# A routed vision tower on one core: routing every five chunks, normalising moved to VectorE, tile 0 fetched within the shared network, padding cut to the ends of the regions

## The chip, the core and the metric

The kernel runs on one core of a Trainium2 chip. The metric is the device time of one execution in microseconds. Before the change three runs gave 1068.31, 1070.25 and 1070.76 us: the median is 1070.25.

## What is computed

64 images of 3 x 96 x 96 are cut into 36 patches each; with a class token that makes 37 tokens of width 256 an image, 2368 in all. Two layers follow (no skip beyond those written):

```
h  = embed(patches) + pos                      # 768 -> 256
h  = h + attn0(norm(h))                        # 16 heads, causal, relative bias
x  = norm(h)
h  = h + shared(x) + sum over the 2 best of 7 experts of w_e * expert_e(x)   # SwiGLU, hidden 704
h  = h + attn1(norm(h))
h  = h + ffn1(norm(h))                         # SwiGLU, hidden 768, int8-like weights
```

The weights w of the two experts are the two largest softmax probabilities, divided by their sum. Everything is held in 32-bit floats; most products are made of three matmuls of an upper and a lower half of each operand (mm3).

## The kernel before, in words

The kernel is a hand-written program for each engine; each engine runs its own list in order, and semaphores join them. Work goes over 8 groups of 8 images (N = 296 tokens). The stages are: embedding; attention(0); ffn(0), the shared network, with the routing woven in; routed(), 43 tiles of 128 routed rows, one expert each; attention(1); ffn(1).

**ffn(0).** A group has six chunks of hidden units (five of 128, one of 64), counted j = 0 to 5. For a chunk, TensorE computes gate and up (gate_up), ScalarE the SiLU (Sg) and later the upper half of the product, VectorE the product (Hd) and the lower half (Hf_lo), and TensorE adds the down product of the chunk two back (LAG = 2). In groups 0 to 6 the routing of the next group, g + 1, is spread over the six chunks: TensorE logits (L1354), token_rows (L1362), counts (L1371); VectorE route (L904, five pieces of small linked operations) and slots_of (L939); ScalarE r_exp and rows, which copy the tokens with their weight into the row buffers rows_x. At the same time the normalisation of group g + 2 runs: mean (TensorE), centre (VectorE), squares (ScalarE), variance (TensorE), deviation (ScalarE, between two activation table loads), norm (L406, GpSimd: xn), then upper_x (ScalarE) and lower_x (L411, GpSimd). The positions are MEAN_AT and VARIANCE_AT (L56).

**The scatter.** For each group GpSimd runs scatter (L485): eight indirect writes of 74 token rows (256 values, the weight, the number of the target row) into routed_in (xs) in DRAM, in the region of each token's expert. A region has room for all tokens. Since a tile of 128 rows may reach past the last row of its expert, SP first fills all of routed_in with rows that count for nothing (L332, nine transfers), behind the loads of the embedding; the first scatter waits for them. In the last group VectorE computes the table of the tiles (table_of_tiles, L1113: expert and first row of each tile) from the counts.

**The queues.** SP's list is: inputs, shared weights, the fill, expert 4 (when the embedding is done), experts 0 to 3 (when attention(0) is done), then a wait for all scatters and the table, then the loads of the tiles (xt, L356), tile t + 2 when tile t has been used. ScalarE issues the loads of experts 5 and 6 and of the weights of attention(1) after tile 0's upper_in (L854 to L856).

**The start of routed().** TensorE waits for the last add to h (L1748), runs six matmuls that compute nothing (keep_going, L1728), transposes tile 0 (tile_in, L1686), and starts its gate and up. Each tile needs the upper half of its expert's weights (ScalarE, upper_weights, L824) and the lower half (VectorE, lower_weights, L1204); their buffers lie over those of the normalisation, so both wait for the end of ffn(0) (norms_idle) and of the scatters (rows_idle). The loop then does, for each tile t: gate and up of half 0, the transpose of tile t - 1's hidden, half 1, tile_in of t + 1, tile_out of t - 1.

```
step(0, 0, True, True, False)                 # over_groups, L286
...
link = linker(RCHAIN * g)                     # route: every operation waits for the one before
```

## Time and profile before

| | us |
|---|---|
| median of three runs | 1070.25 |
| profiled execution, device time | 1067.98 |
| its span | 1066.1 |
| TensorE busy | 982.8 (92%) |
| VectorE busy | 646.8 (61%) |
| ScalarE busy | 624.5 (59%) |
| GpSimd busy | 375.3 (35%) |

The stages in the span: embedding and attention(0) to about 250 us, ffn(0) to 404, the passage and the first tiles to 430, the tiles to 738, then attention(1) and ffn(1). In the profile, PE is TensorE's matmuls and PEld its weight loads, DVE is VectorE, ACT ScalarE, POOL GpSimd, SP the engine that only issues transfers. A row of a timeline has the start, the duration, the engine, the line, the operation, output and inputs, the count, and in brackets how long the engine had been idle before and what released it. The granted clock of TensorE is 1.00 at its upper level (2.4 GHz) and 0.50 at its lower (1.2 GHz).

### The profile page before, as it was taken

Reading aid. Unit: us, or ns where it says so; the run is one execution under the profiler, and the core shown is the slowest. Engines: PE = TensorE matmul, PEld = TensorE weight load, DVE = VectorE, ACT = ScalarE, POOL = GpSimd, SP = SyncE. Lnnn points to the kernel's source line nnn. Section 1 sums busy time; section 2 is a strip of 40 time slices with the busy share of each in tenths; the row PEclk is TensorE's granted clock in tenths of the full one; section 3 lists DMA queues with packets and bytes.
Section 4 is the critical chain, followed back from the end, with each engine's and each line's share of the span. In section 5 each row is a group of like instructions: output and inputs, shape, how many; then the busy total and the mean of one; then the engine's idle time right before and its main releaser. Section 6 shows DMA issues by size and latency. Waiting matters only on the chain.

```text
span 1066.1 us, 28004 instructions
## 1 busy us (share of the span) xinstructions
PE 982.8 (92%) x10628; PEld 891.4 (84%) x10629; DVE 646.8 (61%) x1207; ACT 624.5 (59%) x1077; POOL 375.3 (35%) x295
## 2 busy tenths in 40 slices
PE   4987799988899996999999999999799999899998
PEld 4976688877899995999999999998678888689998
DVE  3635467775666665667667676672467776654543
ACT  3345476864556654565656656653376778655652
POOL 1343334454777770111111111112554654711210
PEclk9998899998999999999999999999899999999999
DMA  6799900005411116011111111111611100000000
GB/s 230 258 246 248 246 17 3 3 3 234 144 35 32 37 37 233 30 40 33 36 35 35 40 35 35 40 34 54 171 26 26 26 2 2 3 13 12 24 24 24
DMA packets 47517, 74.71 MB, mean 70 GB/s; under 512 B 13138, under 2 KB 38994, under 8 KB 46268
## 3 DMA queue, kind: packets, MB, share of 16 engines
q1 hardware_dynamic: 32288, 55.55, 18.7%
q0 software_dynamic: 13328, 10.66, 3.7%
q10 hardware_dynamic: 1804, 7.11, 1.7%
q8 instruction: 72, 1.18, 0.5%
q14 instruction: 25, 0.20, 0.1%
HBM read 41.47 MB, written 31.71 MB: 69 GB/s over the span
## 4 chain that ended last, share of the span: by engine, by line
PE 74%; DVE 6%; issue 6%; ACT 6%; POOL 5%; DMA 3%; SPq 0%; DVEq 0%; ACTq 0%; POOLq 0%
PE ps L1303 24%; PE ps L1308 14%; PE ps L1310 13%; PE ps L1309 13%; POOL routed_in L504 3%; PE ps L1708 3%; PE ps L1452 3%; PE ps L1441 2%; DMA x_in<-in_xT_dram 1%; PE ps L1691 1%; DVE Hd L1103 1%; DVE hsum L1093 1%; DMA xt<-routed_in 1%; ACT RTs L668 1%; ACT RTs L666 1%
## 5 line engine op out<-in xcount | busy, mean ns | idle before, releaser
L1206 DVE TENSOR_TENSOR tile_w<-arena,tile_w 128x1408 fp32r<-128x1408 f32 x86 | 139.5, 1622 | 77.2 <-ACT tile_w L828 77.2
L528 POOL DMA_INDIRECT routed_out<-yt,tile_to x43 | 41.2, 959 | 295.0 <-DVE yt L1228 295.0
L1308 PE MATMUL ps<-tile_w,xTs 128*128 128x352 f32 x344 | 118.8, 345 | 2.6 <-DVE xTs L1211 2.6
L1303 PE MATMUL ps<-arena,shared 128*128 x516 | 120.0, 383 | 1.0 <-ACT shared L822 1.0
L828 ACT ACTIVATE tile_w<-arena 128x1408 fp32r x86 | 118.6, 1379 | 3.3 <-issue 1.5
L1310 PE MATMUL ps<-tile_w,xTs 128*128 128x352 f32 x344 | 111.7, 325 | 0.0
L1309 PE MATMUL ps<-tile_w,xTs 128*128 128x352 f32 x344 | 111.5, 324 | 0.0
L1303 PEld LDWEIGHTS ps<-arena,shared 128*128 128x128 f32 x516 | 95.8, 192 | 12.8 <-issue 1.3
L815 ACT ACTIVATE shared<-ps 128x352 f32<-128x352 f32 x86 | 39.7, 461 | 112.6 <-PE ps L1310 112.6
L398 POOL TENSOR_TENSOR Km<-KT,cst 128x592 f32<-128x592 f32 x64 | 75.6, 1183 | 75.6 <-PE ps L1303 51.8
L969 DVE SCALAR_TENSOR_TENSOR ps<-ps,bias 128x592 f32<-128x592 f32 x64 | 50.1, 783 | 60.2 <-PE ps L1303 60.2
L1103 DVE TENSOR_TENSOR Hd<-Sg,ps 128x296 f32<-128x296 f32 x96 | 44.4, 462 | 68.8 <-ACT Sg L781 67.9
L1308 PE MATMUL ps<-xf_hi,gu_lo 128*128 128x296 f32 x272 | 82.4, 303 | 3.4 <-DVE Hd L1103 2.1
L775 ACT ACTIVATE Hf_hi<-Hd 128x296 fp32r<-128x296 f32 x96 | 43.3, 452 | 71.1 <-DVE Hd L1103 71.1
L1309 PE MATMUL ps<-xf_lo,gu_hi 128*128 128x296 f32 x272 | 81.8, 301 | 0.0
L1310 PE MATMUL ps<-xf_hi,gu_hi 128*128 128x296 f32 x272 | 81.7, 300 | 0.0
L408 POOL TENSOR_TENSOR xn<-cen,rsd 128x592 f32<-128x592 f32 x31 | 45.4, 1463 | 102.1 <-ACT rsd L605 102.0
L654 ACT ACTIVATE prs<-Sb 128x592 f32<-128x592 f32 x64 | 44.7, 698 | 53.9 <-DVE Sb L982 53.8
L1308 PEld LDWEIGHTS ps<-tile_w,xTs 128*128 128x128 f32 x344 | 65.1, 189 | 10.0 <-issue 4.5
L1108 DVE TENSOR_TENSOR Hf_lo<-Hd,Hf_hi 128x296 fp32r<-128x296 f32 x96 | 47.5, 495 | 42.4 <-ACT Hf_hi L775 42.4
L781 ACT ACTIVATE Sg<-ps 128x296 f32<-128x296 f32 x96 | 39.6, 412 | 53.2 <-PE ps L1310 52.3
L1308 PE MATMUL ps<-xa_hi,qkv_p_lo 128*128 128x296 f32 x192 | 66.0, 344 | 2.5 <-DVE h L1010 2.5
(199 smaller groups left out, 2819.0 us busy)
## 6 DMA issues: line engine op xcount, KB each, us to landing
routed_in<-zero_x SPq DMA_DIRECT2D x8, 2064.0 KB, 28.0
arena<-in_ew_dram SPq DMA_DIRECT2D x5, 2176.0 KB, 18.8
x_in<-in_xT_dram SPq DMA_DIRECT2D x7, 888.0 KB, 5.9
xt<-routed_in SPq DMA_DIRECT2D x43, 129.0 KB
arena<-in_ew_dram ACTq DMA_DIRECT2D x2, 2176.0 KB, 10.4
yg<-routed_out SPq DMA_DIRECT2D x8, 512.0 KB
out_dram<-h SPq DMA_DIRECT2D x8, 296.0 KB, 2.7
routed_in<-zero_x SPq DMA_DIRECT2D x1, 1806.0 KB, 27.8
```

Source lines behind the costliest of these rows:

```text
L398: pool.tensor_tensor(Km[p % 2], src, headmask.unsqueeze(1).unsqueeze(3).to_broadcast([P, DK, HG, W2]), ALU.mult).then_inc(a.km, 1)
L408: pool.tensor_tensor(xn[b][:], cen[:], rsd[:].unsqueeze(1).to_broadcast([P, DK, N]), ALU.mult).then_inc(s.xn, 1)
L654: act.activation(Pr[p % 2], Sb[p % 2], ACT.Exp).then_inc(a.ex, 1)
L828: act.activation(tile_w[half][0], gate_up_of(w, half), ACT.Copy).then_inc(s.wh, 1)
L969: dve.scalar_tensor_tensor(out=ps[:, 0:2, 0:DK * HW], in0=ps[:, 0:2, 0:DK * HW], scalar=HD ** -0.5, in1=halves_of(bias[l][:]), op0=ALU.mul ...
L1103: dve.tensor_tensor(Hd[j % (LAG + 1)][0:r], Sg[j % 2][0:r], up, ALU.mult).then_inc(s.hd, 1)
L1108: dve.tensor_tensor(lower, Hd[j % (LAG + 1)][0:r], upper.bitcast(F32), ALU.subtract).then_inc(s.hl, 1)
L1206: dve.tensor_tensor(tile_w[half][1], gate_up_of(w, half), tile_w[half][0].bitcast(F32), ALU.subtract).then_inc(s.wl, 1)
L1303: return pe.matmul(out_, lhsT, rhs, start=start, stop=stop)
L1308: pe.matmul(out_, w[1], x[0], start=start, stop=False)
L1309: pe.matmul(out_, w[0], x[1], start=False, stop=False)
L1310: return pe.matmul(out_, w[0], x[0], start=False, stop=stop)
```

## The change

The routing no longer follows the groups. routing_at(g, j) numbers the chunks of ffn(0) through: routing r (1 to 7) takes chunks 5r - 4 to 5r, one fifth each, so that all are done at chunk 35 of 0 to 47. Within it, the normalisation of group r + 1 runs. norm and lower_x of ffn(0) go from GpSimd to VectorE; GpSimd only scatters, and then issues the loads of experts 5 and 6. The table is computed in group 6; its first piece now also writes ends, the counts as row numbers. The fill becomes six blocks of 128 rows for the spare tiles (five on SP, one on GpSimd) and, when the final counts (ends) are known, seven blocks of 128 rows, each behind the last row of an expert. SP then loads tiles 0 and 1 within the last group; TensorE transposes tile 0 there at j = 3, behind the down product, ScalarE makes its upper half at j = 4, VectorE its lower half at the end. keep_going(6) is gone; the last add to h stands behind the first lower_weights. Cut to its core:

```diff
-MEAN_AT, VARIANCE_AT = (2, 0), (4, 3)
+MEAN_AT, VARIANCE_AT = 0, 3
+PACE = 5
...
+        def routing_at(g, j):
+            at = len(hidden_chunks(I0)) * g + j - 1
+            return (1 + at // PACE, at % PACE) if 0 <= at < PACE * (GROUPS - 1) else (None, None)
@@ SP @@
-            for r in range(0, ROWS, FILL * P):
-                rows = min(FILL, (ROWS - r) // P)
-                sp.dma_start(xs[r:r + rows * P, :].rearrange("(p k) d -> p k d", p=P),
-                             zero_x[:].unsqueeze(1).to_broadcast([P, rows, XW])).then_inc(s_pad, 16)
+            for k in range(1, SPARE):
+                r = EXPERTS * REGION + k * P
+                sp.dma_start(xs[r:r + P, :], zero_x[:]).then_inc(s_pad, 16)
...
-            for scattered in s_scat:
-                sp.wait_ge(scattered, 64 * GROUPS)
+            sp.wait_ge(s_ends, 1)
+            for e in range(EXPERTS):
+                row = sp.value_load(ends[0:1, e:e + 1], min_val=0, max_val=ROWS - P)
+                sp.dma_start(xs[bass.ds(row, P), :], zero_x[:]).then_inc(s_pad, 16)
+            rows_idle(sp)
+            sp.wait_ge(s_pad, 16 * (EXPERTS + SPARE - 1))
+            sp.wait_ge(s_exl, 16)
             sp.wait_ge(s_table, 1)
@@ GpSimd @@
+            def ffn0():
+                pool.dma_start(xs[EXPERTS * REGION:EXPERTS * REGION + P, :], zero_x[:]).then_inc(s_exl, 16)
+                for g in range(GROUPS):
+                    scatter(F[0], g, g % 2)
+                pool.wait_ge(F[0].dn_mm, LAG + 1 + 6 * GROUPS)
+                for e in range(EARLY, EXPERTS):
+                    pool.dma_start(arena[:, e * EW:(e + 1) * EW], ew[e]).then_inc(s_exl, 16)
@@ ScalarE, ffn(0): called with routing_at(g, j) after each chunk @@
+                def routing(r, at):
+                    if at == 2:
+                        sent_before(act, r)
+                        rows(r, r % 2, 0, 7)
+                        if r + 1 < GROUPS:
+                            squares(s, r + 1)
+                    if at == 3:
+                        act.preload_act_table_set("natural_log_exp_and_others")
+                        if r + 1 < GROUPS:
+                            deviation(s, r + 1, 6)
+                        r_exp(r)
+                    if at == 4:
+                        rows(r, r % 2, 1, 7)
...
+                        if l == 0 and last and j == 4:
+                            upper_in(0, 0)
@@ ScalarE, routed @@
                 norms_idle(act)
+                rows_idle(act)
                 w = weights_of(act, 0)
                 upper_weights(0, w, 0)
-                rows_idle(act)
                 upper_weights(0, w, 1)
-                upper_in(0, 0)
-                act.wait_ge(F[0].dn_mm, LAG + 1 + 6 * GROUPS)
-                for e in range(EARLY, EXPERTS):
-                    act.dma_start(arena[:, e * EW:(e + 1) * EW], ew[e]).then_inc(s_exl, 16)
-                act.dma_start(qkv_w1, qkv1).then_inc(s_attw, 16)
-                act.dma_start(out_w1, wo1).then_inc(s_attw, 16)
                 w = weights_of(act, 1)
                 gate(0, 0)
                 upper_weights(1, w, 0)
                 upper_in(1, 1)
                 gate(0, 1)
                 upper_weights(1, w, 1)
+                act.dma_start(qkv_w1, qkv1).then_inc(s_attw, 16)
+                act.dma_start(out_w1, wo1).then_inc(s_attw, 16)
@@ VectorE, ffn(0) @@
+                def norm(g):
+                    dve.wait_ge(s.rsd, FREE + g + 1)
+                    dve.wait_ge(s.cen, FREE + g + 1)
+                    dve.wait_ge(s.xl, g - 1)
+                    dve.tensor_tensor(xn[g % 2][:], cen[:], rsd[:].unsqueeze(1).to_broadcast([P, DK, N]),
+                                      ALU.mult).then_inc(s.xn, 1)
+                def lower_x(g):
+                    x = xf[0][g % 2]
+                    dve.wait_ge(s.xh, g + 1)
+                    dve.tensor_tensor(x[1], xn[g % 2][:], x[0].bitcast(F32), ALU.subtract).then_inc(s.xl, 1)
...
+                def routing(r, at):
+                    if at == 4:
+                        if r + 1 < GROUPS:
+                            norm(r + 1)
+                        slots_of(r, r % 2)
+                    next(routes[r])
+                    if at == 1 and r + 1 < GROUPS:
+                        dve.wait_ge(s.xn, FREE + r + 1)
+                        centre(s, r + 1, 6)
...
+                        if l == 0 and g == GROUPS - 2 and j < TABLE_PIECES:
+                            next(pieces)
+                        if l == 0 and not last and j == 3:
+                            lower_x(g + 1)
@@ VectorE, after ffn(0) @@
-                add_y(GROUPS - 1)
+                if l == 0:
+                    tile_in(0, 0)
...
                 norms_idle(dve)
+                rows_idle(dve)
                 w = weights_of(dve, 0)
                 lower_weights(0, w, 0)
-                rows_idle(dve)
-                tile_in(0, 0)
+                add_y(0, GROUPS - 1)
                 lower_weights(0, w, 1)
@@ TensorE, ffn(0), after gate_up of chunk j @@
+                        if at == 1 and r + 1 < GROUPS:
+                            pe.wait_ge(s.r, RCHAIN * (r - 1) + ROUTE + SLOTS)
+                            mean(s, r + 1, 6)
...
+                        if at == 0:
+                            pe.wait_ge(s.rowB, FREE + r)
+                            logits(r, r % 2, 7)
+                        if at == 1:
+                            pe.wait_ge(s.lg, FREE + r + 1)
+                            token_rows(r, r % 2, 0, 7)
+                        if at == 3:
+                            pe.wait_ge(s.rowA, FREE + r + 1)
+                            token_rows(r, r % 2, 1, 7)
+                            if r + 1 < GROUPS:
+                                pe.wait_ge(s.cen, FREE + r + 2)
+                                variance(s, r + 1, 6)
+                        if at == 4:
+                            pe.wait_ge(s.lnv, FREE + min(r + 2, GROUPS))
+                            counts(r)
+                        if l == 0 and last and j == 3:
+                            pe.wait_ge(s.r, RCHAIN * GROUPS)
+                            tile_in(0, 0, 0)
@@ TensorE, routed @@
-                keep_going(6)
-                tile_in(0, 0, 0)
                 gate_up_half(0, 0, 0)
```

The upper and lower half of tile 0, which lay in the shared network's weights, move to the place of the bias of attention(0).

## Rows read from the trace of the kernel before

**Rows 1.** The chain that ended last, share of the span by engine.

```profile
PE 74%; DVE 6%; issue 6%; ACT 6%; POOL 5%; DMA 3%; SPq 0%; DVEq 0%; ACTq 0%; POOLq 0%
```

**Rows 2.** Windows in attention(0): length; busy of PE, PEld, DVE, ACT, POOL; PEclk, DMA, GB/s.

```profile
120.00:140.00 20.00, 14.85 (x288) 12.07 (x287) 9.61 (x17) 9.51 (x20) 6.44 (x5) 0.91 0.75 189
...
126.00:128.00 2.00, 2.00 (x34) 1.64 (x26) 0.89 (x2) 1.56 (x4) 0.44 (x1) 0.50 1.43 184
...
140.00:160.00 20.00, 19.43 (x398) 16.40 (x398) 14.34 (x25) 14.21 (x28) 9.04 (x7) 1.00 0.01 3
```

**Rows 3.** Timeline of ScalarE, attention(0): the first PTs copy of groups 0, 3 and 4.

```profile
74.26 0.67 ACT L660 ACTIVATE PTs<-ps 74x592 f32<-74x592 f32 x1 [0.82 <-PE ps L1452]
...
149.19 0.67 ACT L660 ACTIVATE PTs<-ps 74x592 f32<-74x592 f32 x1
...
168.68 0.65 ACT L660 ACTIVATE PTs<-ps 74x592 f32<-74x592 f32 x1
```

**Rows 4.** Timeline of TensorE, attention(0): first, longest and last of ten gaps.

```profile
72.81 0.72 PE L1303 MATMUL ps<-Km,QT 64*37 64x148 f32 x16 [1.25 <-issue]
...
124.50 0.67 PE L1303 MATMUL ps<-Km,QT 64*37 64x148 f32 x10 [3.13 <-issue]
133.24 0.25 PE L1303 MATMUL ps<-PTs,cst 74*32 74x74 f32 x1 [1.62 <-issue]
```

**Rows 5.** DMA issues: count, size of each, median us to landing.

```profile
routed_in<-zero_x SPq DMA_DIRECT2D x8, 2064.0 KB, 28.0
```

**Rows 6.** Window of one steady group of ffn(0), columns as in rows 2.

```profile
323.00:342.00 19.00, 19.00 (x146) 18.00 (x145) 11.89 (x39) 11.68 (x21) 14.56 (x13) 1.00 0.17 34
```

**Rows 7.** Timeline of TensorE, ffn(0): the three stalls within it.

```profile
268.13 0.67 PE L1303 MATMUL ps<-rt,cst 74*74 74x28 f32 x8 [1.41 <-DVE rt L927]
...
275.60 1.20 PE L1303 MATMUL ps<-r_w,xn 128*74 128x7 f32 x16 [1.49 <-POOL xn L408]
...
401.36 0.40 PE L1308 MATMUL ps<-Hf_hi,dn_lo 128*128 128x296 f32 x1 [1.07 <-DVE Hf_lo L1108]
```

**Rows 8.** Timeline of the passage from ffn(0) to the tiles.

```profile
403.62 0.30 PE L1310 MATMUL ps<-Hf_hi,dn_hi 128*128 128x296 f32 x1
403.63 1.38 ACT L828 ACTIVATE tile_w<-arena 128x1408 fp32r x1 [1.34 <-issue]
...
405.50 1.62 DVE L1206 TENSOR_TENSOR tile_w<-arena,tile_w 128x1408 fp32r<-128x1408 f32 x1 [0.47 <-ACT tile_w L828]
...
411.03 0.43 PE L1308 MATMUL ps<-tile_w,xTs 128*128 128x352 f32 x1 [1.03 <-DVE xTs L1211]
...
418.51 0.40 PE L1308 MATMUL ps<-tile_w,xTs 128*128 128x352 f32 x1 [1.60 <-DVE xTs L1211]
...
425.65 0.69 PE L1691 MATMUL ps<-cst,xt 128*128 128x128 f32 x2 [2.41 <-DMA xt<-routed_in]
...
430.00 0.51 PE L1308 MATMUL ps<-tile_w,xTs 128*128 128x352 f32 x1
```

**Rows 9.** Timeline of VectorE, ffn(0): a lower half beside a pass of GpSimd.

```profile
265.73 1.94 DVE L1108 TENSOR_TENSOR Hf_lo<-Hd,Hf_hi 128x296 fp32r<-128x296 f32 x1 [0.52 <-ACT Hf_hi L775]
```

**Rows 10.** Timeline of ffn(0), 360 to 372 us: subtraction of the mean, Sg, lower half.

```profile
360.88 0.77 DVE L877 TENSOR_TENSOR cen<-h,ps 128x592 f32<-128x592 f32 x1
...
365.17 0.40 ACT L781 ACTIVATE Sg<-ps 128x296 f32<-128x296 f32 x1
...
371.99 0.48 DVE L1108 TENSOR_TENSOR Hf_lo<-Hd,Hf_hi 64x296 fp32r<-64x296 f32 x1 [0.52 <-ACT Hf_hi L775]
```

**Rows 11.** The scatters by tile (ns min/median/max), and the chain from the last one.

```profile
L504 POOL DMA_INDIRECT routed_in<-prs,slot x32: 1343/1354/1747, 259.1 to 386.3; - x32
...
401.05 5.29 DMA routed_in<-vts,slot
406.34 0.02 SPq L351
...
407.37 2.15 DMA xt<-routed_in
```

## What I expect, and why

> **What bounds the kernel now.** I began with the chain that ended last: TensorE holds 74% of it [rows 1], so time goes only where TensorE waits or runs slowly. I therefore went through the stages and looked for such places.
>
> The first is attention(0). From 120 to 140 us TensorE is busy 14.85 of 20 us and the granted clock is 0.91; from 140 to 160 it is busy 19.43 at a full clock, and the DMA share drops from 0.75 to 0.01 [rows 2]. The PTs copies of ScalarE mark the groups of attention(0): the first starts at 74.26, the fourth at 149.19, the fifth at 168.68 [rows 3]. A steady group thus takes 19.5 us, and the first three took 74.9 where 58.5 would do: 16.4 us are lost. Ten gaps of 0.4 to 3.1 us on TensorE, from 72.81 to 133.24, stand in that stretch with "issue" as releaser: no engine, no data [rows 4]. They sum to 14.3 us, and stretches at the lower of the two clocks (0.50, that is 1.2 GHz) follow them [rows 2]. What fills the DMA engines is the padding of routed_in: eight writes of 2 MB [rows 5] and a ninth, somewhat smaller.
>
> The second place is ffn(0). A steady group takes 19.0 us with TensorE busy throughout [rows 6]. TensorE stalls only at three places: 1.41 and 1.49 us around the first group and 1.07 us at the tail [rows 7].
>
> The third is the passage from ffn(0) to the experts' tiles. The last shared matmul starts at 403.62; tile 0 starts at 411.03, tile 1 at 418.51, tile 2 only at 430.00, after 2.41 us of waiting for its rows [rows 8]. From tile 2 on the loop is full, and the change leaves it alone.
>
> **Part 1, the padding.** 18 MB of writes become 13 blocks of 129 KB; one goes on the GpSimd queue, and seven wait for the final counts. With the DMA engines idle, as from 140 us on, attention runs at 19.5 us a group, so up to 16.4 us return. One gap probably stays: the load of expert 4, until now behind the padding on SP's queue, moves forward to about 70 us, and the last gap (1.62 us) came while that load ran [rows 4]. Sum: -15. Bounds: -9 (the gaps less that one and a low-clock stretch in exchange) to -19 (the first group has no output projection and should take less than 19.5).
>
> What the gaps wait for is not named by the trace. The Trainium skill (Runtime: NRT & Kernel Launch, Instruction fetch mechanics) says that instructions stream in by a DMA queue of the sequencer, in blocks of 16 KiB, at a cost that is "mostly hidden". By its last word this part would give about nothing; that is a rival below. Rows 2 and 4 speak for the gaps going with the traffic.
>
> **Part 2, the rhythm of the routing.** Seven routings of five chunks fill chunks 1 to 35. TensorE's work stays the same: the same logits, transposes, counts, six means and six variances. What can change are its waits.
> Gone: VectorE no longer shares its time with GpSimd's passes. A lower half took 1.94 us instead of 0.47 beside one [rows 9], and this delayed the counts (1.41); the logits' 1.49 was a wait for xn, which GpSimd made behind its scatters [rows 7]. That is -2.9. The table leaves the last group, so the tail's 1.07 shrinks by 0.8.
> New: xn is made on VectorE after the chunk's lower half. Before, this chain ran beside it. From one Sg (365.17) through the table loads to the end of the lower half of the next chunk (372.46) took 7.3 us [rows 10]; with the normalising pass, priced as the 128x592 subtraction (0.77, [rows 10]), 8.1. The copy of rows and the squares in the chunk ahead make ScalarE start some 0.6 late: 8.7. TensorE comes to the next logits after 60 matmuls, at 146 in 19.0 us [rows 6] 7.8 us later. So it waits 0.9 us in each of six rounds, and about 0.8 more in the two where a short chunk lies between; a 128x592 copy for the next x adds some 0.7 in one or two. That sums to 8; the two chunks of lag between gate/up and down absorb part of it, and I take +6. Bounds: 0 (the lag covers all) to +12 (2 us a round, by the larger stalls above).
> VectorE itself fits: of 19.0 us it is busy 11.9 [rows 6]. It gains two 0.77 passes, loses the locked time, and the round shrinks to 16.7 (19.0 less one chunk). GpSimd fits with room: eight scatters at 1.35 and 0.3 between, 13.2 us, and about 2 for the tokens.
>
> **Part 3, tile 0 inside the last group.** The last slots are ready about 6 us after chunk 35's gate/up, as the lower half and nine small VectorE operations must pass. Seven more scatters start within 12 us; the last takes 5.29 to land; SP spends 1.0 on the register loads and the tile 2.15 [rows 11]. That is some 27 us. TensorE reaches the transpose after ten chunks of about 2.5, so it may wait 1.5 us (bounds 0 to 3). SP must also issue the seven blocks, each with a register load, some 7 us, long before the scatters are done: nothing. Transpose and halves lie in the last group: +0.3, inside the tail's stall.
>
> **Part 4, the passage.** TensorE still waits for the last add to h, which now stands behind the first lower_weights. From the last matmul: ScalarE's upper weights 1.4, VectorE's lower 1.6, the two adds 0.8, small starts: tile 0 starts 4.0 after the end, not 7.4 [rows 8]. TensorE sits idle for these 4 us since keep_going is gone, so I expect tile 0 at the low clock for a while, as before. Tile 1 follows 7.5 later as before: its weights, not its rows, set it. Tile 2 follows after a full 7.4 instead of 11.5, because the expert loads now start at the end of ffn(0), on POOL's queue, and are through when xt is asked for. In all 26.4 becomes 18.9: -7.5 (bounds -3.5, the whole 4.1 of tile 2 kept, to -9). The two 1 MB weight loads of ScalarE are issued behind the weights of tile 1, while ScalarE would wait for its gate: nothing, and at most 0.5 if xt shares the engines with them.
> Against this, the Trainium skill (SBUF — State Buffer, two separate sides) says that GpSimd cannot write descriptors of its queue's DMAs while VectorE holds the shared ports; by that the loads on POOL drag on, and tile 2 keeps its wait. The scatters, issued beside VectorE, took 1.34 to 1.75 us each [rows 11]: little.
>
> **Sum**: -15 - 2.9 - 0.8 + 6 + 1.5 - 7.5 = -18.7 us. The profiled execution took 1067.98 us (span 1066.1), 2.3 below the median of the runs, 1070.25; I take the sum off the median: **1051.5 us**. About 0.2% (2.1 us) is what a measurement can tell from no change.
>
> **Rivals.**
> a) The padding is hidden anyway: the gaps belong to the first passes through the code. For: the releaser is only "issue". Against: the fourth to eighth groups run the same instructions without one. Sum -3.7: 1066.5. Chance 0.09.
> b) The expert loads still collide with tile 2: +4.1: 1055.6. Chance 0.13.
> c) The lag covers the longer chain, no new stalls: -6: 1045.5. Chance 0.12.
> d) Slower: VectorE becomes the bound of the routing rounds. Norm, slots, weights and the lower half fall into one chunk; if its serial waits push a round past TensorE's 16.7 us, six rounds lengthen. It decides only from 4.1 us a round, since the other terms give 24.7; at 5 us a round 1070.25 - 24.7 + 30 = 1075.5. Chance 0.03.
> e) Tile 0 does not arrive within the last group: TensorE waits at the transpose with two chunks still to do. At 10 us late: 1060. Chance 0.03.
> The forecast keeps 0.60; its own range is 1045 to 1058.
>
> **Range and chances.** 1042 to 1061 takes in b, c and e and leaves out a, d and the edges. Faster: forecast, b, c, e and nearly all of a, 0.95. Within 0.2%: 0.02. Slower: 0.03.
>
> **What would show it.** Right: PTs copies 19.5 us apart from the first, no "issue" gap over 1 us between 75 and 130 but one; DMA share near 0.1 there; small TensorE waits for xn (line of the new norm) at each logits; the transpose of tile 0 waiting 0 to 3 us for xt; tiles 1 and 2 7.4 apart. Wrong: gaps that stay with idle DMA engines (a); a wait for xt before tile 2 (b); VectorE busy without a break in ffn(0) (d).

## The result and the profile after

The changed kernel takes 1062.66 us (median of 5 runs, 1059.24 to 1063.17), against 1069.01 us (5 runs, 1067.21 to 1070.76) for the kernel before, measured beside it. The ratio is 0.9934, interval 0.9913 to 0.9955. It is faster, since the interval lies below 1, but by about 6.3 us where 18.7 were forecast, and 1062.66 lies above the top of the range, 1061. The profiled execution took 1063.17 us, span 1061.3, mean granted clock 0.975 (before 1067.98, 1066.1, 0.981).

The chain of waits by engine answers [rows 1]: TensorE 72% instead of 74, VectorE 9 instead of 6, ScalarE 9 instead of 6.

```profile
PE 72%; DVE 9%; ACT 9%; issue 5%; DMA 3%; POOL 1%; SPq 0%; DVEq 0%; ACTq 0%; POOLq 0%
```

I cut both spans at the same instructions (the marks) and compared the lengths.

| Stretch | before, us | after, us | difference | forecast |
|---|---|---|---|---|
| start to the first PTs copy | 74.26 | 75.98 | +1.7 | 0 |
| first to fourth group of attention(0) | 74.93 | 59.05 | -15.9 | -15 |
| to the first gate/up matmul of ffn(0) | 101.68 | 103.25 | +1.6 | 0 |
| ffn(0), first gate/up to last shared matmul | 152.75 | 163.28 | +10.5 | +3.8 |
| last shared matmul to tile 2 | 26.38 | 21.22 | -5.2 | -7.5 |
| tile 2 to the end | 636.1 | 638.5 | +2.4 | 0 |
| span | 1066.1 | 1061.3 | -4.8 | -18.7 |

(The forecast for ffn(0) is -2.9 - 0.8 + 6 + 1.5.) The changed kernel's clock is at its lower level (0.50, 1.2 GHz) for some 53 us of the span, against some 40 before.

**Attention(0).** ScalarE's timeline, first PTs copy of groups 0, 3 and 4, answers [rows 3]:

```profile
75.98 0.67 ACT L672 ACTIVATE PTs<-ps 74x592 f32<-74x592 f32 x1 [0.82 <-PE ps L1503]
...
135.03 0.67 ACT L672 ACTIVATE PTs<-ps 74x592 f32<-74x592 f32 x1
...
154.51 0.65 ACT L672 ACTIVATE PTs<-ps 74x592 f32<-74x592 f32 x1
```

The first three groups take 59.05 us, 19.7 each, and the fourth 19.5. TensorE's timeline from 76 to 131 us, all of its "issue" gaps, answers [rows 4]:

```profile
78.27 0.72 PE L1354 MATMUL ps<-Km,QT 64*37 64x148 f32 x16 [0.50 <-issue]
92.59 0.72 PE L1354 MATMUL ps<-Km,QT 64*37 64x148 f32 x16 [1.84 <-issue]
113.29 0.72 PE L1354 MATMUL ps<-Km,QT 64*37 64x148 f32 x16 [0.42 <-issue]
```

Behind the first PTs copy three gaps, 2.8 us, are left, where the kernel before has nine, 13.1 us. (The tenth of [rows 4], 1.25 us at 72.81, stands ahead of that copy, and the changed kernel has it too, at 74.52.) The profile calls them all "issue", but they are of two kinds.

The first kind stands before the first scores matmul of a pair of images (Km,QT). The kernel lets TensorE wait there (a.sc) until VectorE has subtracted the greatest score of the pair before (Sb), and each of these gaps ends 0.10 us after an Sb. For the gap that ends at 92.59:

```profile
91.71 0.78 DVE L999 TENSOR_TENSOR Sb<-ps,mx 128x592 f32<-128x592 f32 x1
```

So these are waits for VectorE. All three above are of this kind, and so are four of the ten of [rows 4] (1.25, 0.50, 1.23, 0.40, together 3.4 us). Attention(1), without any padding, has the 1.84 as well, in both kernels.

The second kind cuts a run of matmuls in the middle, where the kernel has no wait. The kernel before, TensorE's timeline (9 of a run's 16 matmuls, then the gap) and two DMA queues from 92 to 94 us (packets, MB, share of the engines):

```profile
92.29 0.38 PE L1303 MATMUL ps<-PTs,cst 74*32 74x74 f32 x9
94.91 0.35 PE L1303 MATMUL ps<-PTs,cst 74*32 74x74 f32 x4 [2.24 <-issue]
```

```profile
q1 hardware_dynamic: 483, 0.49, 105.8%
q8 instruction: 1, 0.02, 3.5%
```

| Gap of the second kind ends at, us | 85.25 | 94.91 | 103.85 | 111.60 | 124.50 | 133.24 |
|---|---|---|---|---|---|---|
| its length | 1.18 | 2.24 | 1.00 | 1.77 | 3.13 | 1.62 |
| last 16 KB transfer of the instruction queue landed at | 83.86 | 93.35 | 102.25 | 110.25 | 122.93 | 131.78 |

Six gaps, 10.9 us, each end 1.3 to 1.6 us after such a landing. The changed kernel has these transfers too, every 5 to 8 us, and no gap of this kind in attention(0); nor has any other run without the large writes. By these times TensorE waited for instructions that came late beside the writes (four other such landings in that stretch were followed by no gap). The transfers themselves took 0.96 to 1.37 us beside the writes and 0.88 to 1.44 without; what delays them before they start, the trace doesn't tell.

Over the three groups the gaps sum to 10.3 us less than before, and the lower clock level holds 3.4 us instead of 13.7, worth 5.1 at half speed (an estimate): 15.4 of the 15.9 us. The windows there and in the later stages (columns as in [rows 2]):

```profile
80.00:100.00 20.00, 18.16 (x374) 15.16 (x368) 12.91 (x21) 13.72 (x27) 9.36 (x8) 0.91 0.01 3
100.00:120.00 20.00, 19.44 (x416) 16.41 (x408) 14.10 (x24) 14.14 (x28) 8.97 (x8) 1.00 0.01 3
275.00:295.00 20.00, 17.92 (x127) 16.81 (x128) 10.55 (x37) 10.98 (x21) 12.59 (x12) 0.91 0.18 36
315.00:335.00 20.00, 18.68 (x132) 17.52 (x130) 11.79 (x40) 11.77 (x22) 12.04 (x13) 0.91 0.18 37
...
406.00:410.00 4.00, 4.00 (x16) 4.00 (x15) 1.22 (x4) 0.47 (x2) 0.00 (x0) 0.50 1.04 439
414.00:418.00 4.00, 4.00 (x28) 3.98 (x28) 2.27 (x3) 2.08 (x5) 0.00 (x0) 1.00 0.93 312
```

The DMA share at 80 to 120 is 0.01 (before, 0.75 at 120 to 140, [rows 2]). The 1.84 us that stay are not due to the load of expert 4, as I had supposed for the gap that would stay: they are the wait for VectorE shown above.

**ffn(0).** The two windows from 275 and from 315 show what [rows 6] does not: clock 0.91, that is one stretch of 3.41 us at the lower level in each, and a third follows at 356. The kernel before has none there. TensorE's timeline, waits at the logits and in the tail, answers [rows 7]:

```profile
260.96 1.20 PE L1354 MATMUL ps<-r_w,xn 128*74 128x7 f32 x16 [1.30 <-DVE xn L1191]
279.54 1.20 PE L1354 MATMUL ps<-r_w,xn 128*74 128x7 f32 x16 [2.08 <-DVE xn L1191]
299.42 1.20 PE L1354 MATMUL ps<-r_w,xn 128*74 128x7 f32 x16 [1.10 <-DVE xn L1191]
317.54 1.20 PE L1354 MATMUL ps<-r_w,xn 128*74 128x7 f32 x16 [0.94 <-DVE xn L1191]
...
376.23 0.37 PE L1359 MATMUL ps<-Hf_hi,dn_lo 128*128 128x296 f32 x1 [1.22 <-DVE h L1247]
384.90 0.38 PE L1359 MATMUL ps<-xf_hi,gu_lo 128*128 128x296 f32 x1 [1.08 <-DVE Hd L1120]
```

With the waits not shown (0.92 at 354.22 on xn, four of 0.34 to 0.46, and 0.19) they sum to 10.4 us; those of before to 4.4 ([rows 7] and one of 0.38). That is 6.1 us more waiting. The lower clock level holds 12.6 us of the stage (the three stretches, and the end of one that began in attention(0)) against 4.1 before, worth 4.2 us at half speed, an estimate. Together 10.3; 10.5 were measured.

The chain behind the 2.08, VectorE's timeline:

```profile
277.26 0.46 DVE L1120 TENSOR_TENSOR Hd<-Sg,ps 128x296 f32<-128x296 f32 x1 [2.63 <-ACT Sg L798]
278.24 0.47 DVE L1125 TENSOR_TENSOR Hf_lo<-Hd,Hf_hi 128x296 fp32r<-128x296 f32 x1 [0.52 <-ACT Hf_hi L792]
278.63 0.77 DVE L1191 TENSOR_TENSOR xn<-cen,rsd 128x592 f32<-128x592 f32 x1
```

The normalising has its input, rsd, at 275.41, and VectorE is idle for 2.63 us until 277.26; but it stands in the order behind the gate's two operations, which wait for ScalarE. The lower half takes 0.47 and not 1.94 [rows 9], so that gain of the change is real.

**The passage.** TensorE's timeline answers [rows 8]:

```profile
405.41 0.66 PE L1359 MATMUL ps<-tile_w,xTs 128*128 128x352 f32 x1 [3.56 <-DVE h L1247]
413.80 0.40 PE L1359 MATMUL ps<-tile_w,xTs 128*128 128x352 f32 x1 [1.40 <-DVE xTs L1252]
419.98 0.44 PE L1658 MATMUL ps<-cst,xt 128*128 128x128 f32 x2 [1.44 <-DMA xt<-routed_in]
```

Tile 0 starts 3.85 us after the last shared matmul. Its transpose in the last group waits 0.19 us, until 395.11; the last packet of its rows ends at 394.64. It then runs at clock 0.50 (window from 406). The rows of tile 2, asked for at about 414.8, land 5.1 us later, with the DMA engines 0.93 busy (window from 414); a tile took 2.15 in [rows 11]. The expert loads, issued at 402.2 and 402.8, land at 411.4 and 416.8; ScalarE's two loads of the second attention's weights are issued at 412.6 and 413.0. From 414 to 416 the queue of ScalarE's loads holds 0.66 of the DMA engines, that of the experts' 0.27, from 416 to 420 0.48 and nothing.

### The profile page after: what moved, and what is told of

Its sections match the earlier page's. It is cut to its first block, busy times and chain, and to the rows that moved or that the text cites. A ratio compares the mean times of both kernels' runs of the same rounds, so it can differ in the third digit from the quotient of the medians.

```text
span 1061.3 us, 28019 instructions
## 1 busy us (share of the span) xinstructions
PE 984.2 (93%) x10616; PEld 894.0 (84%) x10617; DVE 645.2 (61%) x1221; ACT 623.2 (59%) x1077; POOL 358.6 (34%) x285
## 3 DMA queue, kind: packets, MB, share of 16 engines
q8 instruction: 72, 1.18, 0.5%
## 4 chain that ended last, share of the span: by engine, by line
PE 72%; DVE 9%; ACT 9%; issue 5%; DMA 3%; POOL 1%; SPq 0%; DVEq 0%; ACTq 0%; POOLq 0%
PE ps L1354 24%; PE ps L1359 14%; PE ps L1361 13%; PE ps L1360 13%; PE ps L1759 3%; PE ps L1503 3%; PE ps L1492 2%; DVE Hd L1120 2%; DMA x_in<-in_xT_dram 2%; ACT L798 1%; ACT Hf_hi L792 1%; PE ps L1658 1%; ACT Sg L798 1%; DVE hsum L1110 1%; ACT L812 1%
## 5 line engine op out<-in xcount | busy, mean ns | idle before, releaser
L1354 PEld LDWEIGHTS ps<-arena,shared 128*128 128x128 f32 x516 | 94.7, 190 | 12.5 <-issue 1.3
L1359 PE MATMUL ps<-xf_hi,gu_lo 128*128 128x296 f32 x272 | 86.6, 318 | 4.1 <-DVE Hd L1120 3.7
L1359 PEld LDWEIGHTS ps<-tile_w,xTs 128*128 128x128 f32 x344 | 65.6, 191 | 12.5 <-issue 4.5
L1125 DVE TENSOR_TENSOR Hf_lo<-Hd,Hf_hi 128x296 fp32r<-128x296 f32 x96 | 44.8, 466 | 42.4 <-ACT Hf_hi L792 40.9
L420 POOL TENSOR_TENSOR xn<-cen,rsd 128x592 f32<-128x592 f32 x25 | 36.6, 1466 | 98.8 <-ACT rsd L617 98.8
```

The costliest lines, as they stand in the source:

```text
L1125: dve.tensor_tensor(lower, Hd[j % (LAG + 1)][0:r], upper.bitcast(F32), ALU.subtract).then_inc(s.hl, 1)
L1354: return pe.matmul(out_, lhsT, rhs, start=start, stop=stop)
L1359: pe.matmul(out_, w[1], x[0], start=start, stop=False)
```

## The experiments

Runs that were measured together share their runs of the kernel before; times are medians, ratios are to that. e1 to e4 stood beside 1071.67 us, e5 to e8 beside 1075.58, e9 to e11 beside 1074.08, e12 beside 1070.27. Since that reference moves by 5 us, times of different sets are compared by their ratios, and lengths of stages are compared as well.

**e1, the padding alone.** The kernel before, with the large writes replaced by the thirteen blocks; rhythm, engine of the normalising, and passage are untouched.

```diff
-            for r in range(0, ROWS, FILL * P):
-                rows = min(FILL, (ROWS - r) // P)
-                sp.dma_start(xs[r:r + rows * P, :].rearrange("(p k) d -> p k d", p=P),
+            for k in range(SPARE):
+                r = EXPERTS * REGION + k * P
+                sp.dma_start(xs[r:r + P, :], zero_x[:]).then_inc(s_pad, 16)
...
+            sp.wait_ge(s_ends, 1)
+            for e in range(EXPERTS):
+                row = sp.value_load(ends[0:1, e:e + 1], min_val=0, max_val=ROWS - P)
+                sp.dma_start(xs[bass.ds(row, P), :], zero_x[:]).then_inc(s_pad, 16)
...
-                    pool.wait_ge(s_pad, 16 * FILLS)
```

> The kernel before with only the padding changed: six blocks for the spare tiles and seven at the ends of the regions, all on SP; routing, normalising and passage as before. Theory (the writes of the padding hold up TensorE in attention(0)): the fourth group of attention(0) starts 14 to 17 us earlier than the kernel before (149.19), the gaps with releaser issue between 75 and 130 us are gone but one, and the whole is 12 to 16 us faster, near 1055. Rival (what attention(0) wins is lost again whatever follows, since the changed kernel won only 6): the whole is 5 to 8 us faster. Rival a of the prediction (the gaps are no matter of the padding): within 2 us of the kernel before.

Measured: 1057.77 us (1054.18 to 1063.76), ratio 0.9883 (0.9851 to 0.9915), span 1056.8. The first three groups of attention(0) take 59.1 us. ffn(0) takes 153.5 us, with one stall of 2.14 and 1.09 in the tail, and the passage to the second tile's hidden_t 28.2 (before 28.5). So the padding accounts for the whole gain and more: this kernel's ratio is below the full change's 0.9934, though the two intervals just touch, and its span is 4.5 us shorter.

**e2, the change without its padding part.** The old fill back in the changed kernel, the late blocks out.

```diff
-            for k in range(1, SPARE):
-                r = EXPERTS * REGION + k * P
-                sp.dma_start(xs[r:r + P, :], zero_x[:]).then_inc(s_pad, 16)
+            for r in range(0, ROWS, FILL * P):
+                rows = min(FILL, (ROWS - r) // P)
+                sp.dma_start(xs[r:r + rows * P, :].rearrange("(p k) d -> p k d", p=P),
+                             zero_x[:].unsqueeze(1).to_broadcast([P, rows, XW])).then_inc(s_pad, 16)
...
+                pool.wait_ge(s_pad, 16 * FILLS)
```

> The changed kernel with the old fill of all of routed_in and without the seven late blocks. Theory: attention(0) has its gaps back, and the whole is 12 to 17 us slower than the changed kernel, 6 to 10 slower than the kernel before (1075 to 1079): the rest of the change then costs time by itself. Rival (gains don't add): about as the changed kernel, 1062.

Measured: 1074.69 us (1073.13 to 1079.31), ratio 1.0035 (1.0009 to 1.006), span 1072.1. The gaps are back, at DMA share 1.10. Its window, columns as before, and three of its ten "issue" gaps on TensorE between 76 and 142 us (together 12.0 us):

```profile
80.00:100.00 20.00, 15.35 (x294) 12.79 (x293) 11.60 (x19) 11.87 (x23) 7.88 (x6) 0.91 1.10 249
```

```profile
91.57 0.72 PE L1353 MATMUL ps<-Km,QT 64*37 64x148 f32 x16 [1.23 <-issue]
95.11 0.27 PE L1353 MATMUL ps<-PTs,cst 74*32 74x74 f32 x4 [2.52 <-issue]
109.38 0.47 PE L1502 MATMUL ps<-cst,prs 64*74 64x64 f32 x5 [1.94 <-issue]
```

The code is that of the changed kernel, first passes included, so rival a falls: the gaps of the second kind come and go with the traffic. There are six in mid-run here, 8.9 us, two of them shown (95.11 and 109.38); each ends 1.3 to 1.6 us after a 16 KB transfer of the instruction queue has landed, and so, 1.2 us after one, does a seventh gap, 1.02 us ahead of an output product. The 1.23 is of the first kind. The first three groups take 70.7 us here, not 74.9, so from this side the padding is worth 11.7 us there. Everything else together made the kernel slightly slower: ffn(0) takes 162.9 us, and its five waits for xn and three clock stretches are those of the changed kernel (1.28, 2.08, 1.11, 0.92, 0.92).

**e3, the normalising one chunk earlier on VectorE.**

```diff
                     if at == 4:
-                        if r + 1 < GROUPS:
-                            norm(r + 1)
                         slots_of(r, r % 2)
                     next(routes[r])
+                    if at == 3 and r + 1 < GROUPS:
+                        norm(r + 1)
```

> The changed kernel with VectorE's norm one chunk earlier, behind the fourth piece of the routing, where VectorE stands idle for 2.6 us until the next Sg (and rsd lies ready). Theory (TensorE's waits in ffn(0) come from norm's place behind the next lower half): the five waits for xn (1.30, 2.08, 1.10, 0.94, 0.92) go, and with them some of the stretches at the low clock; ffn(0) shrinks from 163.6 to 153 to 157 us, the whole to 1052 to 1057. Rival (ScalarE's two table loads or VectorE's load are the bound of the round): the waits move to Hd or the rows, the whole stays within 2 us of 1062.

Measured: 1056.45 us (1051.66 to 1058.06), ratio 0.9861 (0.9832 to 0.989), span 1054.0. ffn(0) takes 156.3 us instead of 163.3. Two rows of TensorE at the logits, and two windows of the rounds:

```profile
261.30 1.23 PE L1354 MATMUL ps<-r_w,xn 128*74 128x7 f32 x16 [0.86 <-ACT vts L632]
279.52 1.23 PE L1354 MATMUL ps<-r_w,xn 128*74 128x7 f32 x16 [1.71 <-ACT prs L632]
```

```profile
267.00:287.00 20.00, 18.29 (x141) 17.34 (x140) 12.62 (x44) 11.24 (x20) 13.08 (x12) 1.00 0.19 38
302.00:322.00 20.00, 19.41 (x147) 18.20 (x146) 13.15 (x46) 11.67 (x21) 13.98 (x12) 1.00 0.19 38
```

The five waits at the logits shrink from 6.3 to 4.3 us, and now end with ScalarE's second copy of token rows out of bank 7 (L632), which the logits overwrite. That copy is a limit that the sum had not named. The three clock stretches are gone, worth 5.1 us. Together 7.2, against 7.0 measured: the larger part of the gain is the clock, not the wait. The link holds in most runs: the changed kernel, e2 and e6 have the same waits and three stretches each, e3 and e12 the shorter waits and none; but e10, with the same ffn(0) as e3, has one, behind the first logits.

**e8, the normalising back on GpSimd,** behind each scatter, in the changed kernel.

```diff
                 for g in range(GROUPS):
                     scatter(F[0], g, g % 2)
+                    if g + 2 < GROUPS:
+                        pool.wait_ge(F[0].xl, g + 1)
+                        norm(F[0], g + 2, g % 2)
...
-                        if r + 1 < GROUPS:
-                            norm(r + 1)
                         slots_of(r, r % 2)
```

> The changed kernel with norm back on GpSimd, behind the scatters of the routing before; lower_x stays on VectorE. Tests the part 'VectorE normalising'. Theory (GpSimd's eight scatters fill most of a round, so norm on it comes late): waits of TensorE for xn of 1 to 3 us in each of the six rounds, VectorE operations held to 1.5 us and more beside norm, ffn(0) 163 to 170 us, the whole 0 to 7 us slower than the changed kernel. Rival (norm on VectorE is what costs): the waits go as in e3, the whole 3 to 6 us faster than the changed kernel.

Measured: 1059.77 us (1054.48 to 1060.77), ratio 0.9843 (0.9808 to 0.9877), span 1058.5, ffn(0) 158.2. Of its waits one is for xn (1.54 us); four are for ScalarE's copy (1.72, 0.75, 0.57, 0.56). So the rival holds in the main, not the theory. At the place where the change puts it, the normalising was better off on GpSimd; only a chunk earlier is VectorE as good.

**e5, ScalarE's copy earlier too:** e3 with rows(r, r % 2, 1, 7) taken from at == 4 to right behind r_exp(r) at at == 3. **e11** is the same edit in e8.

> As e3_norm_earlier (norm one chunk earlier), and ScalarE copies the second half of the token rows right behind its exponentials, before it reloads the SiLU table, not one chunk later. In e3 the five waits before the logits had turned into waits for that copy (0.86, 1.71, 0.68, 0.51, 0.50), since the logits take the same bank. Theory (ScalarE's order of work, not its load, holds the logits): the five waits go, ffn(0) shrinks from 156.3 to 151 to 154 us, the whole to 1050 to 1055. Rival (ScalarE's load: the copy, the two table loads and four more passes in one chunk): the wait moves on to Sg and Hd, ffn(0) stays over 155 us.

> Changed kernel with the normalising back on GpSimd behind each scatter, and with ScalarE's second copy of the token rows out of bank 7 moved a chunk forward. With the normalising alone on GpSimd feed-forward 0 was 158.2 us with waits for that copy of 1.72, 0.75, 0.57 and 0.56 us. Theory (those waits are the next limit and VectorE, free of the normalising, has room): they go, feed-forward 0 at 154.5 us, total about 1056. Rival (ScalarE's copy so early delays its own exponentials and the routing behind them, as it did with the normalising on VectorE, where the waits went elsewhere): feed-forward 0 at 158 us or more, total 1060 or more.

Measured: e5 1059.34 us (1057.19 to 1061.96), ratio 0.9848 (0.9818 to 0.9879), ffn(0) 163.3. e11 1063.43 us (1061.52 to 1070.19), ratio 0.9909 (0.9876 to 0.9943), ffn(0) 166.2. Both times the rival holds: the waits for the copy at the logits go (in e11 two for xn stay, 1.56 and 0.69), and others come, behind ScalarE's copy at another place, VectorE's routing and its later add to h. In e11, TensorE's timeline:

```profile
300.52 0.63 PE L1418 MATMUL ps<-cst,xn 128*74 128x128 f32 x4 [0.79 <-DVE rt L929]
324.66 0.63 PE L1418 MATMUL ps<-cst,xn 128*74 128x128 f32 x4 [1.52 <-ACT vts L635]
333.10 0.37 PE L1359 MATMUL ps<-Hf_hi,dn_lo 128*128 128x296 f32 x1 [1.70 <-DVE h L1247]
```

So the copy's place is a wait that is passed on, not one to be had for nothing.

**e9, filler at the logits.** It asks how much of the loss is the clock: TensorE works where it would wait.

```diff
                             pe.wait_ge(s.rowB, FREE + r)
+                            for _ in range(2):
+                                mm(ps[:, 7, 0:2 * P], ident, cst[:, 0:2 * P])
                             logits(r, r % 2, 7)
```

> Changed kernel, with four full-width matmuls of nothing (about 0.9 us, into bank 7, overwritten by the logits) put on TensorE between its wait for rowB and its wait for xn, once in each of seven groups. It tells the stalls themselves from the clock that they cost. Theory (the stalls at the logits leave TensorE idle long enough that the 0.50 stretches of 3.41 us at about 281, 319 and 356 follow, and these cost three times 1.7 us): the waits for xn are shorter by the filler, the stretches in the last stage of the front part are gone, and feed-forward 0 goes from 163.3 us to about 158; total about 1058. Rival (the granted clock does not depend on these stalls, or the filler only takes its own time): the three stretches stay, feed-forward 0 is 163 to 167 us, total 1062 to 1066.

Measured: 1064.1 us (1058.31 to 1067.91), ratio 0.9899 (0.9862 to 0.9935), span 1061.6, ffn(0) 163.1. Of the three clock stretches one stays (at 279 us), behind this wait, which the filler follows and cannot fill:

```profile
276.90 1.13 PE L1354 MATMUL ps<-cst 128*128 128x256 f32 x4 [1.71 <-ACT prs L632]
277.87 1.17 PE L1354 MATMUL ps<-r_w,xn 128*74 128x7 f32 x16
```

```profile
300.00:350.00 50.00, 48.49 (x357) 45.14 (x356) 29.00 (x100) 29.90 (x53) 33.84 (x28) 1.00 0.18 36
```

From 300 to 350 us the clock is full, where the changed kernel has one stretch at 0.50. The clock half of the theory holds in two of three places; the forecast time does not. The filler takes seven times 0.95 us and replaces only some 2 us of waits for xn (the wait for the copy, 0.90, 1.71, 0.76, 0.55, 0.55, stands ahead of it): +4.6. The lower clock level holds 3.4 us of the stage instead of 12.6 (besides the two stretches, the piece at its start is missing), worth 4.6 us. Filler work costs as much as it brings here.

**e4, filler in the passage; e10, the same in e3.**

```diff
             ffn(0)
+            keep_going(7)
             pe.wait_ge(F[0].y, FREE + 2 * GROUPS)
```

> The changed kernel with seven matmuls that compute nothing on TensorE between the last down product of ffn(0) and the wait for the last add to h. Theory (the idle 3.6 us there cost a stretch at the low clock in tile 0): tile 0 and 1 run at the full clock, tile 2 starts 1.5 to 3.5 us earlier, the whole is 1 to 4 us faster than the changed kernel. Rival (the granted clock there does not hang on these 3.6 us): no change beyond 1 us.

> Changed kernel with the normalising moved to the chunk before on VectorE (as in the run that did this alone) and with the 14 full-width matmuls of nothing between the last shared matmul and tile 0. If the two are independent: feed-forward 0 at 156 us, tile 0 at the full clock, its hidden_t 12.4 us behind the last shared matmul instead of 14.1, of which the wait for tile 2's rows takes some 0.9 back; total about 1055.5, 1 us below the run with the normalising alone. Rival (the wait for the rows of tile 2 takes all of it, since they land by the transfers and not by TensorE): no difference from 1056.5 or up to 1 us more.

Measured: e4 1061.28 us (1059.81 to 1063.3), ratio 0.9911 (0.9885 to 0.9938). e10 1055.53 us (1054.24 to 1060.08), ratio 0.9838 (0.9808 to 0.9867), span 1054.1. In e10:

```profile
396.25 0.43 PE L1359 MATMUL ps<-tile_w,xTs 128*128 128x352 f32 x1 [0.53 <-DVE h L1247]
402.82 0.40 PE L1359 MATMUL ps<-tile_w,xTs 128*128 128x352 f32 x1 [2.26 <-DVE xTs L1252]
410.21 0.44 PE L1658 MATMUL ps<-cst,xt 128*128 128x128 f32 x2 [2.64 <-DMA xt<-routed_in]
```

Tile 0 keeps the full clock and comes to its hidden_t 12.4 us after the last shared matmul instead of 14.3; then the waits before tile 1 and for tile 2's rows grow from 1.40 and 1.44 (changed kernel) to 2.26 and 2.64. hidden_t of tile 1 comes 22.7 us after it, where e3 has 23.2. The spans of e10 and e3 are equal and the intervals overlap: whether the filler brings that half microsecond is not settled. In e4 the stretch from the last shared matmul to tile 2 is 1.0 us shorter than in the changed kernel, and ffn(0), which the edit leaves alone, some 2 us longer, with 18.0 us at the lower clock instead of 12.6.

**e6, expert loads behind the rows of tile 2; e7, this with e5 and e4.**

```diff
                 pool.wait_ge(F[0].dn_mm, LAG + 1 + 6 * GROUPS)
+                pool.wait_ge(s_xt[0], 32)
```

> The changed kernel, but GpSimd issues the loads of experts 5 and 6 only when the rows of tile 2 have landed. Theory (rows of tile 2 took 5.1 us to land because the expert loads share the DMA engines): the wait of 1.44 us before tile 2 goes, tile 2 starts 1.5 to 3 us sooner after the last shared matmul, the whole is 1 to 3 us faster than the changed kernel. Rival (the two weight loads on ScalarE's queue are what they share with): the wait stays over 1 us.

> e5, e6 and the filling matmuls of e4 together. If the parts add: e5's gain in ffn(0), 1.5 to 3 us from tile 2's rows and 1 to 2 us from tile 0 at the full clock: 1047 to 1052, faster than both kernels. Rival (parts compete for the same slack): about as e5.

Measured: e6 1068.32 us, ratio 0.9937 (0.9913 to 0.9961); e7 1067.58, 0.9927 (0.99 to 0.9954); spans 1068.5 and 1069.6, against the changed kernel's 1061.3. By its ratio e6 is no slower than the changed kernel (0.9934). The wait before tile 2 is gone, hidden_t of tile 1 comes 21.7 us after the last shared matmul instead of 23.4, and one tile later stands this (e6, then e7):

```profile
431.29 0.69 PE L1659 MATMUL ps<-cst,xt 128*128 128x128 f32 x2 [6.20 <-DMA xt<-routed_in]
```

```profile
431.92 0.69 PE L1658 MATMUL ps<-cst,xt 128*128 128x128 f32 x2 [6.55 <-DMA xt<-routed_in]
```

The rows of tile 2 took 3.0 us (asked for at 413.8, there at 416.85, when GpSimd's wait for them was released), now beside ScalarE's loads alone, against 5.1 beside both. So the expert loads cost those rows 2.1 us, more than the whole wait of 1.44; moved one tile on they make one four times as long.

**e12, ScalarE's loads late.** e10 with the two loads for the second attention issued at the last tile but one.

```diff
                 def step(t, b, last):
+                    if isinstance(t, int) and t == TILES - 2:
+                        act.dma_start(qkv_w1, qkv1).then_inc(s_attw, 16)
+                        act.dma_start(out_w1, wo1).then_inc(s_attw, 16)
...
-                act.dma_start(qkv_w1, qkv1).then_inc(s_attw, 16)
-                act.dma_start(out_w1, wo1).then_inc(s_attw, 16)
                 over_tiles(act, step)
```

> The kernel of the run with the earlier normalising and the filler in the passage, with ScalarE's two loads of the second attention's weights (1 MB together) issued at the last tile but one instead of behind the weights of tile 1. It tells which transfers make the rows of tile 2 late. In the changed kernel those rows took 5.1 us to land, in a stretch where ScalarE's loads moved most (0.66 of the DMA engines at 414 to 416, the experts' loads 0.27), and 3.7 us beside ScalarE's loads alone. If ScalarE's loads hold the larger part: the wait before tile 2, 2.64 us without this edit, goes to 1.2 us or less, hidden_t of tile 1 comes 21.3 us behind the last shared matmul instead of 22.7, total about 1054. If the experts' loads hold it: the wait stays above 2 us, and the total at 1055.5. If the loads at their new place meet the gather at the end of the tiles, the passage gains and the total is 1056 or more.

Measured: 1052.2 us (1046.46 to 1056.55), ratio 0.984 (0.9806 to 0.9874), span 1048.8. Time and span are the shortest of all; the ratio is that of e10 (0.9838), since the kernel before ran 3.8 us faster beside it. TensorE's timeline, to be read against the last rows of e10:

```profile
405.35 0.40 PE L1360 MATMUL ps<-tile_w,xTs 128*128 128x352 f32 x1 [2.24 <-DVE xTs L1253]
410.68 0.44 PE L1659 MATMUL ps<-cst,xt 128*128 128x128 f32 x2 [0.59 <-DMA xt<-routed_in]
```

The wait before tile 2 falls from 2.64 to 0.59 us, and hidden_t of tile 1 comes 20.7 us after the last shared matmul, not 22.7. The rows took 4.2 us to land, beside the expert loads alone, where e10 has 6.3 beside both. So ScalarE's loads cost them 2.1 us, as much as the expert loads did in e6. The first expectation holds by its number; that ScalarE's loads hold the larger part does not follow. At their new place, from 697 us, the end of the tiles does not lengthen.

## Why the forecast was too large

**Part 1 was right in kind and size.** -15 forecast, -15.9 in the marks; alone it gave a ratio of 0.9883 (e1), and its absence 11.7 us of attention(0) (e2). Its bound of -19 was not neared. Two readings in it were wrong. The ten gaps of [rows 4] were not all of one kind: 3.4 of the 14.3 us are waits for VectorE, which no change of traffic removes, and the gap that stays is one of them, not the load of expert 4. And the later groups do have "issue" gaps (0.43 us in each, of the same kind), where rival a was argued against by their having none. Besides, the groups are written out one by one in the program, so that the later ones are first passes too. What the other 10.9 us wait for is shown by their times only: each ends 1.3 to 1.6 us after a transfer of the instruction queue. The rule "mostly hidden" of the Trainium skill (Runtime: NRT & Kernel Launch, Instruction fetch mechanics) would have given nothing here; the trace does not agree with it beside this traffic, and e1 and e2 decide against it.

**Part 2 is the step that failed.** ffn(0) came to +10.5, not +3.8. Of the 6.7 us in excess 4.2 are the clock, for which the sum had no term, and 2.3 are waits (6.1 measured, 3.8 forecast). In its terms:
- "-2.9": the counts' wait of 1.41 went, but the logits' 1.49 did not. It changed its releaser from GpSimd to VectorE (1.30 and 2.08).
- "-0.8": the tail's 1.07 did shrink, to 0.34. But two new waits, 1.22 at 376.23 and 1.08 at 384.90, stand in group 6, where VectorE now makes the last slots, the table and the add to h and never pauses for more than 0.6 us from 370 to 388 us. The sum moved the table there for nothing.
- "+6": the waits at the logits, +6.3, are the size forecast, for a reason only half seen. e3 shows 4.3 of them under the wait for ScalarE's copy of rows in bank 7; the chain of xn adds just 2.0 on top.
- No term was given to the clock. The three stretches at 0.50 within ffn(0) cost 5.1 us (half of 3 x 3.41, an estimate; 4.2 is the balance with the pieces at the start of the stage), and e3, which shortens the waits by 2.1, has none of them. I had priced such a stretch in part 1, as one of its losses, and not where I forecast a wait in every round.

**Part 3.** The transpose waited 0.19 us and not 1.5, inside the bounds of 0 to 3. The last packet of its rows ended 0.47 us before it started (0.44 and 0.41 in e7 and e6, which waited 0.77 and 0.30), so it was most likely the wait for them, and the chain ended just about when TensorE got there.

**Part 4.** -5.2 instead of -7.5. Tile 0 started at 3.85 as forecast (4.0). Tile 1 followed 8.4 us later, not 7.5, since tile 0 ran at the low clock; tile 2 followed 9.0 later, not 7.4. The wait, 1.44 us, is rival b at a third of its price, with two sources of equal size. The rows of tile 2 took 2.1 us less without the expert loads beside them (e6), and 2.1 less without the two loads of ScalarE (e12 against e10), which I had booked at "nothing, and at most 0.5". I had asked what ScalarE would have to wait for, and not what the rows of tile 2 would meet. The expert loads on POOL's queue were hardly dragged on: 9.2 and 14.0 us to landing, against 8.0 and 12.8 on ScalarE's queue before, about 1.2 us more, though in other company. That is little for the Trainium skill's rule on the shared ports (SBUF — State Buffer, two separate sides), which I had weighed against the change.

**What had no term.** The start and the end of attention(0) took 3.3 us more and the rest after tile 2 took 2.4 us more, mostly by low-clock stretches in code the change doesn't touch: the lower level holds 6.8 and 7.9 us of the first two (before 3.4 and 2.7) and 15.1 of the last (before 9.0). TensorE's waits of over 0.15 us there are as before (in the last 24.8 us, before 25.0). e1, e3 and e10 place such stretches differently again. Why they fall where they do stays open.

**The rivals.** a and e fell, and c did too; b came in part. d named the right engine and the right order of its work, but ffn(0) as a whole grew by 10.5 us, 1.5 for each of seven rounds, where it needed 4.1. Put right, the sum is -15.9 + 10.5 - 5.2 + 1.7 + 1.6 + 2.4 = -4.9, and the medians give -6.3.

**A better version.** The padding carries the change. With the normalising a chunk earlier, filler in the passage and ScalarE's loads late, e12 has a span 12.5 us below the changed kernel's and 8.0 below e1's, and beats the kernel before and the changed one: 1052.2 us, ratio 0.984. The intervals of e1, e3, e8, e10 and e12 overlap, so of its steps only the stage lengths say what each brings: 7.1 us in ffn(0) and 2.7 from the last shared matmul to tile 2. Another 3.2 us stand behind tile 2 (2.0 in the rest of the tiles, the others with a shorter time at the lower clock), where none of its steps should act; they aren't explained.

## What to carry to other kernels

Bulk writes of padding are not free because no one waits for them: here they took 12 to 16 us from an engine that used none of their data. Where a step is moved onto an engine that runs in order, look for what it stands behind there, and for every reader of the same bank, as the wait that is second today is the limit tomorrow. Where a profile names no releaser, look for the wait in the kernel, and for the engine's instructions among the DMA queues, before you put all such gaps down to one cause. And price each new short wait twice in a kernel bound by TensorE, as a wait and by the clock stretch that may follow it; and each transfer that is moved by what it will share the DMA engines with.

## What the runs showed of the chip

- Five waits of 0.92 to 2.08 us at the logits came with three stretches at clock 0.50, 3.41 us each (changed kernel, e2, e6); waits of 0.5 to 1.7 us at the same places came with none in e3 and e12 and with one in e10.
- A tile of 129 KB took 2.15 us to land by itself [rows 11], 3.0 beside loads of 768 and 256 KB (e6), 4.2 beside a load of 2.1 MB (e12), and 5.1 (changed kernel) and 6.3 (e10) beside both.
- In attention(0) TensorE stopped in the middle of runs of matmuls six times under the padding writes (10.9 us), in e2 also six times (8.9 us), each stop ending 1.3 to 1.6 us after a 16 KB transfer of the instruction queue had landed, and never without the writes.
